# Reordering a graph layer: the mix beside the edge maxima, the attention beside the output rows

## The reference

```python
xn = _layernorm(x)
x = x + gnn(xn, edges) + mix(xn)
x = x + ffn(_layernorm(x))
# gnn: x1 = relu(xn @ W_ah + b); three graph attention layers on x1, each with 4 heads of 192:
h = (x1 @ W).reshape(N, H, C)
e = leaky_relu(as_n[src] + ad_n[dst], 0.2)
m = segment_max(e, dst); p = exp(e - m[dst]); alpha = p / segment_sum(p, dst)
out = segment_sum(alpha * h[src], dst) + b        # relu, the three joined, then @ W_out
# mix: 12 heads of 64, 256 random features
data_dash = (64 ** -0.25 * data) @ proj.T         # data = q or k
k_prime = exp(dash_k - diag_k - max over all heads, nodes and features) + 1e-4
q_prime = exp(dash_q - diag_q - max over its features) + 1e-4
out = q_prime @ (k_prime.T @ v) / (q_prime @ sum(k_prime))   # then @ w_proj
# ffn: 8 experts with 195 places each, gelu, chosen by a softmax
```

## Time and profile before

| | |
|---|---|
| median of three executions | 1930.38 us |
| the profiled execution | 1942.82 us |
| its span on the core | 1941.1 us |
| PE busy | 1617.9 us, 83% |
| DVE busy | 1201.9 us, 62% |
| ACT busy | 606.2 us, 31% |
| POOL busy | 515.7 us, 27% |
| mean granted TensorE clock | 0.927 |

### The profile page before, as it was taken

One profiled execution on the slowest core, in us unless ns is written; L12 is line 12 of the kernel. 1 busy time (PEld: TensorE's weight loads), 2 busy tenths in 40 slices (PEclk: granted clock), 3 DMA queues, 4 the chain that ended last, 5 costly groups with the idle time before them and its releaser, 6 DMA issues.

```text
span 1941.1 us, 24679 instructions
## 1 busy us (share of the span) xinstructions
PE 1617.9 (83%) x9663; PEld 1203.3 (62%) x9663; DVE 1201.9 (62%) x2553; ACT 606.2 (31%) x1194; POOL 515.7 (27%) x282
## 2 busy tenths in 40 slices
PE   3899997999167769999898998889998998973993
PEld 2456664555044347888787887877786665643662
DVE  7667632024138959998999986868775344763113
ACT  2221101122121144646464665433322121431110
POOL 1487787777400000212021021212212000002002
PEclk9999998999578989999999999999998999976997
DMA  7424434343332160426241332144323224406725
GB/s 215 112 43 117 113 58 103 60 82 66 62 123 70 62 204 24 135 72 163 83 125 46 100 99 83 54 153 158 109 70 119 72 96 152 172 8 226 245 67 183
DMA packets 197362, 208.90 MB, mean 108 GB/s; under 512 B 83041, under 2 KB 152815, under 8 KB 197245
## 3 DMA queue, kind: packets, MB, share of 16 engines
q1 hardware_dynamic: 117453, 183.36, 29.1%
q0 software_dynamic: 76416, 14.38, 6.2%
q10 hardware_dynamic: 3375, 9.59, 1.9%
HBM read 140.67 MB, written 66.22 MB: 107 GB/s over the span
## 4 chain that ended last, share of the span: by engine, by line
PE 39%; DVE 24%; DMA 14%; POOL 11%; issue 7%; ACT 3%; SPq 1%; another core or an unknown queue 0%; ACTq 0%; POOLq 0%; DVEq 0%
DMA table<-amount,place 11%; PE bank L891 10%; POOL table L1877 9%; PE bank L740 6%; PE bank L741 5%; PE bank L742 5%; DVE eb L1318 5%; DVE eb L1327 4%; DVE junk L1282 4%; PE bank L1049 3%; PE bank L1037 3%; DVE q_max L1350 2%; PE bank L916 1%; PE bank L945 1%; DVE qf L1367 1%
## 5 line engine op out<-in xcount | busy, mean ns | idle before, releaser
L891 PE MATMUL bank<-hb,eb 128*128 128x193 f32 (+3 forms) x2400 | 430.4, 337 | 18.1 <-DVE eb L1327 16.0
L891 PEld LDWEIGHTS bank<-hb,eb 128*128 128x128 f32 (+3 forms) x2400 | 408.7, 194 | 31.8 <-DVE eb L1327 22.9
L1877 POOL DMA_INDIRECT table<-amount,place x170 | 344.2, 2025 | 146.6 <-DMA table<-amount,place 54.4
L1888 POOL TENSOR_TENSOR node<-node,rinv 128x960 f32<-128x960 f32 (+2 forms) x36 | 63.3, 1771 | 839.1 <-DVE rinv L1340 839.1
L1690 ACT ACTIVATE eb<-eb,asd 128x640 f32<-128x640 f32 (+1 forms) x240 | 183.1, 812 | 313.8 <-DVE eb L1318 313.4
L1318 DVE SCALAR_TENSOR_TENSOR eb<-shift_b,as_low,shift_b 128x640 f32<-128x640 f32 (+1 forms) x240 | 233.7, 1015 | 8.4 <-DMA shift_b<-shift_rows 8.4
L1327 DVE SCALAR_TENSOR_TENSOR eb<-eb,count 128x1280 f32<-128x1280 f32 (+1 forms) x120 | 200.4, 1670 | 1.0 <-ACT eb L1690 1.0
L1282 DVE CUSTOM_DVE_ANT_0 junk<-ab,absent 128x1250 bf16<-128x1250 f32 x120 | 177.7, 1481 | 1.4
L740 PE MATMUL bank<-w_o_hi,aT_hi 128*128 128x384 bf16 (+1 forms) x480 | 160.4, 334 | 0.4 <-DVE won L1505 0.4
L741 PE MATMUL bank<-w_o_lo,aT_hi 128*128 128x384 bf16 (+1 forms) x480 | 160.6, 335 | 0.0
L742 PE MATMUL bank<-w_o_hi,aT_lo 128*128 128x384 bf16 (+1 forms) x480 | 160.0, 333 | 0.0
(11 more groups left out here) (249 smaller groups left out, 2830.5 us busy)
## 6 DMA issues: line engine op xcount, KB each, us to landing
w<-in_w SPq DMA_DIRECT2D x16, 1152.0 KB, 8.4
shift_b<-shift_rows SPq DMA_DIRECT2D x24, 625.0 KB, 6.8
h_rows<-h_row SPq DMA_DIRECT2D x27, 388.0 KB
hb<-h_rows SPq DMA_DIRECT2D x12, 873.0 KB
ar<-node_rows SPq DMA_DIRECT2D x27, 384.0 KB, 3.1
qk_rows<-qk_row SPq DMA_DIRECT2D x12, 625.0 KB
ab<-as_rows SPq DMA_DIRECT2D x12, 625.0 KB, 5.1
stage<-in_W SPq DMA_DIRECT2D x18, 384.0 KB, 4.4
```

The costliest lines, as they stand in the source:

```text
L891: ins = T.matmul(bank[w // 2][0:M, c0:c0 + GC + 1], p[0:K, u, w * P:w * P + M], hv[0:K, t, 0:GC + 1], start=opens and u == 0 and w % 2 == ...
L1877: G.indirect_dma_start(tables[i], bass.IndirectOffsetOnAxis(place[:, c:c + 1], axis=0), amount16[:, c:c + 1], None, compute_op=ALU.add).th ...
L1888: ins = G.tensor_tensor(v, v, rinv[0:R, half, ws].unsqueeze(2).broadcast_to([R, ws.stop - ws.start, GC]), ALU.mult)
```

## The change

The count waits for 64 rounds instead of 80 at rate 1.6, and it runs in step: the table of tile t, the transposition of tile t-1 and `absent` of tile t-2 in one round, where they stood behind each other before. The key maxima of the last pair move behind the last projections, and `pair_in` of the first pair ahead of them; `pair_in` no longer waits for the key maximum and for all stores, but for its own pair's. The edge maxima of layers 0 and 1 run at 0.9 per round beside the rest of the projections and the mix. The attention starts when the mix is over: two items per round, with two edge maxima of layer 2 per round as long as there are any, beside the weights and rows of block 0, then of block 1. The weights of block 1 are no longer loaded with the rows of block 0 but in 8 rounds of their own behind them. Tiles move in SBUF to allow this, and w1_in and w2_in of expert 3 move ahead of `ranked`, with other waits. A `yield None` at the end of each round of `paced` lets one `paced` run inside another.

```diff
-COUNT_RATE, MIX_RATE, EDGE_RATE = 1.6, 1.0, 1.3
-COUNT_DELAY = 80
+FIRST_EDGE_RATE, LATER_RATE = 0.9, 2
+COUNT_DELAY = 64
@@ paced
                     live.remove(track)
                     break
+        yield None
@@ projection_steps
-        if n % 2 == 0:
-            for t in range(NT):
-                yield "k_top", NT * (n // 2) + t
-                if t % 2:
-                    yield None
+        if n % 2 == 0 and n // 2 < PAIRS - 1:
+            yield from k_tops(n // 2)
     yield "norms", NC * 2 * PAIRS - 1
+    yield "pair_in", 0
+    yield from k_tops(PAIRS - 1)
     yield "top", 0
     yield None
+def k_tops(pair):
+    for t in range(NT):
+        yield "k_top", NT * pair + t
+        if t % 2:
+            yield None
+
-def count_steps():
+def graph_steps(done):
     for _ in range(COUNT_DELAY):
         yield None
-    for t in range(NT):
-        yield "count", t
+    yield from in_step([(0, lambda t: [("count", t)]), (2, lambda t: [("absent", t)]),
+                        (1, lambda t: [("count_turn", t)])], NT)
+    yield "ab_in", 0
+    yield from paced((itertools.chain(edge_layer(0), edge_layer(1)), FIRST_EDGE_RATE))
+    while "mix" not in done:
         yield None
-    yield "ab_in", 0
-    yield from edge_layer(0)
+    yield from paced((attention_steps(), LATER_RATE), (last_edges(done), LATER_RATE))
...
-def edge_steps():
-    for l in range(1, LAYERS):
-        yield from edge_layer(l)
+def last_edges(done):
+    yield from edge_layer(LAYERS - 1)
+    done.add("edges")
@@ mix_steps
-        if pair == PAIRS - 1 and kind != "k":
-            yield from weight_step(0, n - (len(order) - KD - 2))
+        if pair == PAIRS - 1 and kind == "q" and b == 0:
+            yield "head_in", 0
...
+    done.add("mix")
     yield "mix_bias", 0
-    yield None
+    for i in range(KD + 2):
+        yield from weight_step(0, i)
+        yield None
...
     def load(u):
         yield "row_in", u
-        yield from weight_step(1, u)
...
                         (2, project)], NT)
+    while "edges" not in done:
+        yield None
+    for i in range(KD + 2):
+        yield from weight_step(1, i)
+        yield None
@@ last_order
+    yield "w1_in", 3
+    yield "w2_in", 3
     yield "ranked", 0
...
-    for i in (3, 4):
-        yield "w1_in", i
-        yield "w2_in", i
+    yield "w1_in", 4
+    yield "w2_in", 4
@@ whole_order
-    yield from paced((projection_steps(), 1), (count_steps(), COUNT_RATE))
-    yield from paced((attention_steps(), 1), (mix_steps(), MIX_RATE), (edge_steps(), EDGE_RATE))
+    done = set()
+    yield from paced((itertools.chain(projection_steps(), mix_steps(done)), 1), (graph_steps(done), 1))
@@ sync_program
             def pair_in(pair):
-                second_over()
+                sy.wait_ge("qk_mm", NC * 2 * PAIRS)
+                for i in range(2):
+                    sy.wait_ge(f"qk_out{i}", 16 * (pair + 1))
+                    sy.wait_ge(f"v_out{i}", 16 * HALF)
```

More of the change, by code:

```diff
@@ L1 @@
+import itertools
 from contextlib import ExitStack
@@ L255, in mix_order, with mix_steps @@
             for kind, n in (("k", SPLITS), ("q", SPLITS), ("", 3)) for b in range(n)]
-def mix_steps():
+def mix_steps(done):
     order = mix_order()
@@ L518, in program @@
         cursor[0] = r_a
-        w_o = [[put(f"w_o0_{p}", [128, KD, D], BF16) for p in ("hi", "lo")]]
-        ar = [put(f"ar{i}", [P, D]) for i in range(2)]
-        aT = [[put(f"aT{i}_{p}", [128, KD, P], BF16) for p in ("hi", "lo")] for i in range(2)]
+        w_o = [[put(f"w_o1_{p}", [128, KD, D], BF16) for p in ("hi", "lo")]]
+        ar = [[], [put(f"ar{i}", [P, D]) for i in range(2)]]
+        aT = [[], [[put(f"aT{i}_{p}", [128, KD, P], BF16) for p in ("hi", "lo")] for i in range(2)]]
         assert cursor[0] <= r_b
[L523 to L528, removed]
         cursor[0] = r_a
@@ L539, in program @@
         xnT = [put(f"xnT_{p}", [128, KD, N], BF16) for p in ("hi", "lo")]
+        assert cursor[0] <= r_c
+        cursor[0] = r_b
+        ar[0] = [put(f"mix_ar{i}", [P, D]) for i in range(2)]
+        aT[0] = [[put(f"mix_aT{i}_{p}", [128, KD, P], BF16) for p in ("hi", "lo")] for i in range(2)]
+        bp = put("bp", [P, D])
+        xr = [put(f"xr{i}", [P, D]) for i in range(2)]
         assert cursor[0] <= r_c
@@ L593, in program @@
         cursor[0] = r_d
-        w_o.append([put(f"w_o1_{p}", [128, KD, D], BF16) for p in ("hi", "lo")])
+        w_o.insert(0, [put(f"w_o0_{p}", [128, KD, D], BF16) for p in ("hi", "lo")])
+        assert cursor[0] <= after_features
+        cursor[0] = r_d
+        pr, ro = put("pr", [P, N]), put("ro", [P, N])
+        mate, won = put("mate", [P, N], BF16), put("won", [P, N], BF16)
+        even, win = put("even", [P, P], BF16), put("win", [P, P], BF16)
+        cnt = put("cnt", [P, 3, NT])
+        signs = put("signs", [P, 2], BF16)
         assert cursor[0] <= after_features
@@ L624, in program @@
         att = [put("att0", [P, NT, 128]), att1]
+        cursor[0] = r_f
+        st2 = [put(f"st2_{i}", [128, D]) for i in range(2)]
         shift = put("shift", [P, NT, TURN])
@@ L642, in program @@
         orow += [put(f"orow{i}", [128, D]) for i in (2, 3)]
-        cursor[0] = r_g
-        bp = put("bp", [P, D])
-        xr = [put(f"xr{i}", [P, D]) for i in range(2)]
         cursor[0] = r_g
@@ L973, in row_mm @@
                     pe.wait_ge("out_lo", KD * block + k + 1)
-                    ins = three(bank[row_bank(i)][0:R, 0:HROWS], [a[:, k, 0:R] for a in aT[u % 2]],
+                    ins = three(bank[row_bank(i)][0:R, 0:HROWS], [a[:, k, 0:R] for a in aT[u >= NT][u % 2]],
                                 [w[:, k, cs] for w in ws], k == 0, k == KD - 1)
@@ L1053, in tensor_program @@
             mine = dict(keys_turn=keys_turn, turn=turn, x1=x1, h=h, as_rows=as_rows_, v=v, qk=qk, norms=norms, k_top=k_top, top=top_,
-                        count=count_, gather=gather, dash=dash, k_sum=k_sum, q_turn=q_turn, q_out=q_out,
+                        count_turn=count_turn, gather=gather, dash=dash, k_sum=k_sum, q_turn=q_turn, q_out=q_out,
                         row_turn=row_turn, row_mm=row_mm, f_turn=f_turn, logits=logits,
@@ L1572, in vector_program @@
                         w_part=w_part, x1=x1, h=h, as_rows=as_rows_, same=same_, place=place_, feats_in=feats_in, qk=qk, norms=norms,
-                        k_top=k_top, top=top_, count=count_, edge_max=edge_max, shifts=shifts, weigh=weigh,
+                        k_top=k_top, top=top_, count=count_, absent=absent_, edge_max=edge_max, shifts=shifts, weigh=weigh,
                         finish=finish, q_exp=q_exp, q_feat=q_feat, divide=divide, out_split=out_split,
@@ L2134, in w2_in @@
                 i = e % WEIGHT_SETS
[L2135 removed]
+                if e == 4:
                     slots_over()
```

42 lines of the change are left out of this document (17 added, 25 removed), and 2 rows, old and new, of the table TAKEN_OVER.

## The result

The changed kernel takes 2048.5 us (2044.45 to 2057.25 in four runs). The kernel before took 1936.3 us in the four executions compared with it. The ratio is 1.056 with a 95% interval of 1.0527 to 1.0594. The forecast was 1890, in a range of 1850 to 1950, with the kernel before at 1930.4; its fourth execution moved that median to 1936.3. The profiled execution took 2048.93 us with a span of 2047.2, 106 more than the 1941.1 before.

A forecast was written before the change was run, and what follows sets the result against it. PE and DVE were taken to starve in turn. Mix at 614, plus 252 and 609, gave attention over at 1475 and block 2 at 1584 against 1624: -40, so 1890 from a median of 1930.4, range 1850 to 1950.

The forecast's parts named there:

- What bounds the kernel now: Whole kernel: PE and DVE starve in turn; PE idles 36.5 us before the count and waits 13.6 for keys.
- Part 1: Start until the mix begins: projections to 589, plus counts 14, edge maxima 6, global maximum 5; mix at 614, against 709.
- Part 2: Mix beside 70 edge maxima without attention: 42 us a pair, 252 us in all, over at 866.
- slots slide over each other by up to five: Mix: overlap of slots allows 34.6 to 45 us a pair; the query chain gives most back, so 42.
- the mix becomes a chain: Rival for the mix alone: query slots of 6.5 us unhidden, 58 a pair, +98, total 1988; chance 0.12.
- the ring: Mix query slots: chain of `dash`, maxima, shift, features, transposition, next `dash`, each waiting for the last; 6.5 us a slot unhidden.
- the lists are rigid: Mix: reason for taking 42 us a pair, near the slot sum of 42.7 from each slot's longest engine.
- the clock rival: Rival for DVE-bound attention rounds: PE clock falls to 1.2 GHz, +16 and +68, total 1974; chance 0.06.
- Part 3: Attention beside rows: DVE-bound rounds 235, then 202, 66 and 106 us; sum 609, over at 1475.
- the loss of 1.26 per half: PE-bound attention rounds: 1.26 us lost per half row, since DVE waits for it before preparing the next item.
- The rule on POOL and DVE: Attention finishes: the skill's blocking rule read as about 5 us lost each, sum 8 to 13 higher; 3.4 by the row taken.
- Everything behind block 2: Block 3, routing and experts: same steps, 317 us to the end as before; expert 3's earlier weight load taken as 0.

The follow-up runs named there:

- c1: Changed kernel with `absent` of tile t-2 ahead of the count of tile t in each round; 2041.9 us.
- m1: Changed kernel with the mix's division behind the exponentials and features in each slot instead of ahead of them; 2010.2 us, ratio 1.035 to the kernel before.
- b0: Kernel before the change, with the mix's division moved behind the exponentials and features; 1948.9 us, ratio 1.0034.
- r1: Changed kernel with DVE taking each half of an output row (blocks 0 to 2) out of PSUM one round later; 2026.1 us.
- a2: Changed kernel with division last, late eviction and `absent` first, plus attention and last edge maxima at 1.3 per round instead of 2; 1954.5 us.
- a1: Changed kernel with three edits together (division last, late row eviction, `absent` ahead of the count), order of stages otherwise kept; 1974.0 us.
- b2: Changed kernel with the three edits; attention joins the mix early at 0.75 a round, edge maxima at 2, later 1.0; 1895.8 us, ratio 0.976.
- b3: Changed kernel with b2's early, spread attention but without the three edits; 1941.6 us, ratio 1.0013 to the kernel before.
- s1: First part of the change alone (earlier count, late key maxima, early load), then attention, mix and edge maxima side by side as before; 1956.7 us, ratio 1.0068.

## Why the prediction was wrong

*What bounds the kernel now* was read rightly: the hole at the count and the wait for the keys are gone. The last projection ends 68 us and the mix begins 70 us earlier than before.

*Part 1*, 614 forecast, 640 measured. The mis-sized term is that of the count, 14 us for ten counts. With the last key maxima taken off (8.3 us by the earlier trace rows), the sum has the last projection at 595; it is at 623.9, so the counts cost 43, more than the upper end of 34 that I had taken from the stall of before. I priced the additions and the transpositions, and took the waits among DVE, ACT and PE for hidden; how much of the 43 is the low clock of that stretch (0.77) is open. In step means that the three stages of three tiles share a round; in one engine's list they still stand in an order, and `absent` stood behind the count. c1 took 14 of the 29 back.

*Part 2* is the step that failed. I wrote that "slots slide over each other by up to five" and took 42 us per pair; a pair takes 55 (331.8 / 6). The mechanism was among the rivals, "the mix becomes a chain", at 58 per pair, with a chance of 0.12; even its total of 1988 lies 60 us below the measured one. Two of my arguments for that low chance were wrong. First, I looked for the ring in the query slots, where `dash` and the maxima are; those run at 3.3 to 4.2 us as summed. It closes behind them. The last query slot and the three empty ones, 14.3 us in my sum, take 16.2 to 21.6, and the first two key slots of the next pair, 6.1 in my sum, take 9.1 to 12.7. In that chain I left out the reciprocal, 0.17 us of work that stands first in DVE's list: its wait counts, not its work. m1 shows it. Second, "the lists are rigid" should have meant that a slot sum of the longest engines is a lower end, not an upper one: it holds only if no engine waits for another inside a slot. And the clock rival I put into the attention at 0.06, where it hardly came (0.89, DVE-bound as forecast); the half clock came in the mix, where the waits are, with some 30 of the 80 us by the estimate above.

The trace of before did speak for it: in the earlier trace rows PE waits 23.3 us for the features even with a gather between. b0 and m1 together show the rule behind it: the same order of stages costs 38 us without a neighbour and nothing with one.

*Part 3*, 609 forecast, 637 measured. The DVE-bound rounds were right (228 us for 235, by the first instructions of the items). The 21 rounds of block 0 after them took 210 us for 202, the 8 weight rounds 74 for 66, and the last 11, with block 1, 123 for 106. I took the loss of 1.26 per half over from before and added no loss for a second item in the round and for a DVE that also waits; r1 puts 18 us on the eviction's position. a2 took another 19.5 back with a more even pairing, which I had seen (PE-bound here, DVE-bound there, rows alone at the end with DVE at 25 of 66) without drawing the conclusion. The tail was 14 us longer, in the rest of block 1, from 1608 to 1665.

*The rule on POOL and DVE.* The two DVE instructions of the items take these sums now:

```profile
L1332 DVE SCALAR_TENSOR_TENSOR eb<-shift_b,as_low,shift_b 128x640 f32<-128x640 f32 (+1 forms) x240 | 247.4, 1072 | 0.0
L1341 DVE SCALAR_TENSOR_TENSOR eb<-eb,count 128x1280 f32<-128x1280 f32 (+1 forms) x120 | 200.2, 1668 | 0.0
```

Together 447.6 us. Undisturbed, the half of the 120 items that is 610 wide takes 3.03 and the half that is 640 wide 3.16, which makes 371. The 76 us between are 3.2 for each of the 24 finishes, against 3.4 by the row; the kernel before lost 62 us in the same way, so that the disturbance grew by 14 in the new order. The price of about 5 was not what the rule gives. The Trainium skill, SBUF — State Buffer, "Who interferes with whom", has the later of the two instructions wait until the other is over. The trace of the kernel before agrees: in the earlier trace rows `weigh` starts at 813.73, under POOL's instruction of 813.23 to 815.75, and ends at 817.04, 1.29 us after that one, where it takes 1.42 undisturbed. What is lost is the part of POOL's instruction that is left when DVE's starts, and not both of POOL's instructions whole.

*Sum.* 26 + 80 + 28 + 14 = 148 us against the forecast. The three edits together took back 74 (a1), and the even order another 78 (b2). *Everything behind block 2* cost the same, as said; expert 3's earlier load shows in nothing.

What stays open: the 39 us by which the mix of m1 still lies above the forecast, which the rows put on the shorter ring and the half clock that is left without a run that takes them apart; and why the clock falls in some drains and not in others behind the same wait.

## What to carry to other kernels

Before a stage is taken away from its neighbour, follow its waits through one slot of each kind, the drains too, with the engines' lists side by side, and count instructions of 0.2 us that stand first in a list: if the chain returns to its start, the slot costs the sum of its members, and it is the neighbour that made it cheap. The place of a short instruction in the order can be worth more than its stage (38 us for one moved stage here, none for 100 us of load taken away). Look at the granted clock of such a stretch as well: here the waits of the ring cost less by their length than by the half clock behind them. And pair heavy stages so that every round has its share of each engine: the even spread was worth 107 us here (b3), and the rebuilt start by itself nothing (s1).

## What the runs showed of the hardware

The same 16 records of a 65-column float32 product took 1.90 us and, in the changed kernel's second drain, 3.52 after a wait of 2.33. The same wait stood in all six drains of that run, and the product behind it took 3.5 us in three, 2.75 in one and 1.90 in two: the wait does not decide alone. A stretch with PE at 266 of 332 us busy by the records had a clock of 0.84, and the busy time itself contains the slow products, so that a busy share says little on how loaded PE is. Twelve idle products of 512 columns behind each q_out brought the next ones back to 1.92 and 1.90: with 2.6 us more of work, the stretch from the second to the third q_out took 4.4 us instead of 4.8. Without idle products and at the full clock it took 3.2. A DVE instruction with two inputs in SBUF that began while GpSimd scaled the sums ended only behind GpSimd's instruction (817.04 against 815.75 in the earlier trace rows); that cost 3.2 us in each of 24 finishes.
